# Four blocks of transformer layers on one core: a GpSimd wait moved three fetches later, long VectorE steps cut in pieces, and a static plan with other durations

## The chip, the cores and the metric

The kernel runs on one core of a Trainium2 chip. The metric is the device time of one launch in microseconds (us). Weights are rearranged on the host before the launch and are not timed. The core's engines are TensorE (PE in the rows), VectorE (DVE), ScalarE (ACT), GpSimd (POOL) and the queue of SyncE (SP), which only issues DMAs. Each engine runs its own list of instructions in order and waits on semaphores for the others.

## The reference

The input `x` has 2 x 1024 tokens of 256 features; a context has 2 x 154 tokens. Four layers follow each other, and each is a cross-attention and a feed-forward block, both with a layer norm in front and a residual sum behind:

```python
x = x + xattn0(ln(x), ctx);  x = x + ffn0(ln(x))   # ternary weights with a low-rank term
x = x + xattn1(ln(x), ctx);  x = x + ffn1(ln(x))   # 32 fetched expert rows per token, and a gated MLP
x = x + xattn2(ln(x), ctx);  x = x + ffn2(ln(x))   # rotary attention; 8 routed and 2 shared experts
x = x + xattn3(ln(x), ctx);  x = x + ffn3(ln(x))   # auto-correlation attention; 8 experts, top 2
```

Two parts matter here. In ffn0 the weights are made ternary on the chip:

```python
scale = clip(mean(abs(w), axis=1), 1e-5)
w_t = clip(round(w / scale), -1, 1) * scale
h = x @ w_fc_t.T + gate * (x @ v.T @ fast_b.T @ u.T);  y = relu(h) ** 2 @ w_proj_t.T
```

In ffn1 each token picks, for 4 heads, 8 of 4096 experts by two small top-8 searches, and then sums over its 32 experts:

```python
ew = silu(hidden . down_embed[indices]) * softmax(scores);  y = sum(ew * up_embed[indices])
```

## The kernel before, in words

The 2048 tokens are 4 chunks of 512, and a chunk is 4 tiles of 128 tokens (the partitions). All of `x` stays in SBUF as `x_sb`. The function `plan()` writes a list of work items for each engine: every item has an engine, a name, an assumed duration and the items that it needs. A list scheduler then goes through assumed time. When an engine is free it takes, of its items that are ready, the one with the longest remaining chain, and that order is the order in which the engine's instructions are written. Nothing is reordered on the chip. The table `DUR` holds assumed durations by item kind and overrides those in the `add` calls; an item kind that is not in it keeps the duration of its call. An item is never interrupted.

Items that the change touches:

- `tern`: ffn0's weights. VectorE makes them in three items. `tern(0)` (assumed 9 us) computes the scales and four of the 128-row blocks of `w_fc`, `tern(1)` (6 us) the other four, `tern(2)` (16 us) the two blocks of `w_proj`, and then adds the low-rank term to `w_fc` in eight steps, each after a TensorE product (L905) and a VectorE add (L1542). `tern(3)` is TensorE's 32 transposes with ScalarE's eight evictions (L920, L1264). The first product of ffn0, `h0(0,0)`, needs all eight evictions.
- `p1`: 16 short steps of an attention chunk, a TensorE product (L814) and a VectorE maximum (L1497) for each. TensorE may be two of them ahead. The attention's exponentials wait for the last one.
- `tk1` and `ix1` (`top1`, `rows1`, L1571 to L1603): VectorE's last steps of the routing of a chunk in ffn1. `ix1` is one item of 13.5 us, and ends with `rowid`, the indices, and `prob`, the weights.
- The gather. A unit `g` is 4 of the 32 expert rows of a tile of tokens; a chunk has 32 units, and there are 128 in all. Their rows go to a ring of 5 slots (20 rows of 2 x 256 values). For each unit GpSimd issues four indirect DMAs (`gf`, L1803), VectorE multiplies the first halves by the hidden state (`mu`, L1369), ScalarE sums each row (`th`, L1161), VectorE forms the four weights (`ew`, L1376 and L1377), VectorE adds the first three weighted rows to `x_sb` (`ad`, L1386 to L1388), ScalarE scales the fourth row (`sc`, L1170) and GpSimd adds it to `half_sum` (`ad`, L1817, or a copy, L1814). After eight units VectorE adds `half_sum` to `x_sb` (`ga`, L1394).
- `bo`: GpSimd adds an attention bias to the four tiles of a chunk (L1823).

A slot is refilled by `fetch(g)`. Before the first of its four DMAs GpSimd waits for VectorE's `ad` of unit g-5 (`f1_acc`, L1800) and for its own `ad` of that unit (`f1_half`, L1801). The item of GpSimd's own `ad` stands ahead of the fetch on the same engine, most often directly.

The chunks run in the order `A_ORDER`, (layer, chunk): (0,0), (0,1), (1,0), (1,1), (0,2), (0,3), (1,2), (1,3), (2,0) to (2,3). The gather of chunks 0 to 3 lies beside the attention and ffn of the chunks behind.

Of the kernel before, what the change touches and what calls it, by code (L numbers as in the profile page):

```python
# [10 lines left out]
P = 128  # L11
B, T, D = 2, 1024, 256
# [42 lines left out]
def columns(pack):  # L55
# [24 lines left out]
    DVE=dict(kv=3.2, N1=2.6, N3=1.0, p1=0.85, t=0.7, y=0.45, h0=0.78, y0=0.45, sm1=4.3, gu1=0.72, tk1=5.2, ix1=13.5, mu=1.27,  # L80
             ew=0.45, ad=1.7, ga=0.45, Q=6.2, lg2=5.5, gu2=0.72, y2=1.95, ks3=3.0, vs3=3.0, tp=4.0, y3=0.95, l3=1.2, lg3=7.0,
             be3=2.0, u3=1.1),
    POOL=dict(bo=3.1, gf=4.3, ad=0.82, bo3=6.0))
SIGNAL, LAND, BIAS_LATER = 0.22, 5.0, 10.0
# [3 lines left out]
LAST = NCH - 1  # L88

def plan():
# [113 lines left out]
    def ffn0(c, xt, prev):  # L205
        for m in range(8):
            p = add("PE", ("h0", c, m), 1.7, xt, *prev, c == 0 and ("ACT", ("tern", 3)), m > 1 and ("ACT", ("h0", c, m - 2)),
                    m and ("PE", ("h0", c, m - 1)))
            sq = add("ACT", ("h0", c, m), 1.3, p)
        use["xtf"] = p  # L210
        for i in range(TI):
            p = add("PE", ("y0", c, i), 3.2, sq, i > 1 and ("DVE", ("y0", c, i - 2)), i and ("PE", ("y0", c, i - 1)))
            out = add("DVE", ("y0", c, i), 0.43, p)
        return (out,)

    def ffn1(c, xt, prev):
# [11 lines left out]
        t2 = add("DVE", ("ix1", c), 13.0, a, c >= 2 and ("DVE", ("ga", UNITS * (c - 1) - 1)))  # L228
# [208 lines left out]
def build(nc, io):  # L437
# [10 lines left out]
    with ctx:  # L448
# [3 lines left out]
        def sem(name):  # L452
            return ctx.enter_context(nc.semaphore(name))
# [83 lines left out]
        def vrest(b):  # L537
# [27 lines left out]
        tn_w, tn_z, tn_zs, tn_u, tn_nat, tn_tp, tn_ev = (  # L565
            sem(s) for s in ("tn_w", "tn_z", "tn_zs", "tn_u", "tn_nat", "tn_tp", "tn_ev"))
# [166 lines left out]
        def _(eng):  # L733
# [162 lines left out]
            def tern(r):  # L896
                if r == 2:
                    eng.wait_ge(ld_f0, 16)
                    eng.wait_ge(tn_w, 1)
                    mm(psum[0:RANK, 6, 0:D], f0("fbt")[0:RANK, :], f0("v")[0:RANK, :], start=True, stop=True).then_inc(tn_z, 1)  # L900
                    eng.wait_ge(tn_zs, 1)
                    for m in range(8):
                        if m >= 2:
                            eng.wait_ge(tn_nat, m - 1)
                        mm(psum[:, 6 + m % 2, 0:D], utg[0:RANK, m * P:(m + 1) * P], lowv[0:RANK, :],  # L905
                           start=True, stop=True).then_inc(tn_u, 1)
                if r == 3:
                    eng.wait_ge(tn_nat, 8)
                    for t in range(8):
                        if t >= 2:  # L910
                            eng.wait_ge(tn_ev, t - 1)
                        for z in range(4):
                            if t < 4:
                                kt, m = t // 2, 4 * (t % 2) + z
                                src = fcnat[:, m, kt * P:(kt + 1) * P]
                            else:
                                mo = 4 * (t - 4) + z
                                m, o = mo // 2, mo % 2
                                src = projnat[:, o, m * P:(m + 1) * P]
                            ins = eng.transpose(psum[:, 6 + t % 2, z * P:(z + 1) * P], src, ident)  # L920
                        ins.then_inc(tn_tp, 1)
# [201 lines left out]
            def experts3(c, y):  # L1123
# [11 lines left out]
                for kt in range(KT):  # L1135
# [5 lines left out]
                    "w": weigh, "t": turn_back, "o": turn_out, "y": project_out, "tern": tern, "h0": hidden0, "y0": out0,  # L1141
# [8 lines left out]
        def _(eng):  # L1150
# [100 lines left out]
            def tern(r):  # L1251
# [3 lines left out]
                if r == 3:  # L1255
                    for t in range(8):
                        eng.wait_ge(tn_tp, t + 1)
                        if t < 4:
                            kt, m = t // 2, 4 * (t % 2)
                            dst = fc_t[:, kt, m * P:(m + 4) * P]  # L1260
                        else:
                            m = 2 * (t - 4)
                            dst = proj_t[:, m:m + 2, :].rearrange("p m n -> p (m n)")
                        act(dst, bank(6 + t % 2), ACT.Copy).then_inc(tn_ev, 1)  # L1264
# [93 lines left out]
        def _(eng):  # L1358
# [156 lines left out]
            def scales():  # L1515
                eng.wait_ge(ld_f0, 16)
                own.mark(eng.tensor_reduce(absum[:, 0:8], fcnat, AX.X, ALU.add, apply_absolute_value=True))
                own.link(eng.tensor_reduce(absum[:, 8:10], projnat, AX.X, ALU.add, apply_absolute_value=True))
                own.mark(ts(sclip[:, 0:8], absum[:, 0:8], 1.0 / D, 1e-5, ALU.mult, ALU.max))
                own.link(ts(sclip[:, 8:10], absum[:, 8:10], 1.0 / HID0, 1e-5, ALU.mult, ALU.max))  # L1520
                own.mark(ts(hi_th, sclip, 0.5, None, ALU.mult))
                own.link(ts(lo_th, sclip, -0.5, None, ALU.mult))
# [8 lines left out]
            def tern(r):  # L1531
                if r == 0:
                    scales()
                    ternary(range(0, 4))
                if r == 1:
                    ternary(range(4, 8))
                    ts(utg[0:RANK, :], utg[0:RANK, :], f0("gate")[0:RANK, :], None, ALU.mult).then_inc(tn_w, 1)
                if r == 2:
                    ternary(range(8, 10))
                    for m in range(8):  # L1540
                        eng.wait_ge(tn_u, m + 1)
                        tt(fcnat[:, m, :], fcnat[:, m, :], psum[:, 6 + m % 2, 0:D], ALU.add).then_inc(tn_nat, 1)  # L1542
# [37 lines left out]
            def rows1(c):  # L1580
                n = 16
                ex = ex1.rearrange("p (r k) -> p r k", r=n)
                for r in range(n):
                    own.mark(eng.max_index(pos[:, r * 8:r * 8 + 8], best[:, r, :], sums[:, r].rearrange("p i j -> p (i j)")))
                own.wait()
                own.mark(ts(pside[0], pos, 3, None, ALU.logical_shift_right))
                own.link(ts(pside[1], pos, 7, None, ALU.bitwise_and))
                for z in range(2):
                    own.mark(eng.tensor_copy(psidef[z], pside[z]))
                own.wait()  # L1590
                for z in range(2):
# [3 lines left out]
                    own.link(eng.reduce_sum(pick[z], eq.rearrange("p r k j -> p (r k) j"), AX.X))  # L1595
                own.link(stt(rowf, pick[0], float(NKEY), pick[1], ALU.mult, ALU.add))
                if c >= 2:
                    eng.wait_ge(f1_tile, TI * (c - 1))
                ts(rowid[c % 2][:, :], rowf, float(NEXP1 - 1), None, ALU.min).then_inc(f1_idx, 1)
                eng.wait_ge(f1_se, c + 1)  # L1600
                own.link(eng.reduce_sum(esum, ex, AX.X))
                own.link(eng.reciprocal(erec, esum))
                tt(prob[c % 2][:, :].rearrange("p (r k) -> p r k", r=n), ex, cast(erec.unsqueeze(2), [P, n, 8]), ALU.mult).then_inc(f1_idx, 1)  # L1603
# [153 lines left out]
            def experts3(c, y):  # L1757
# [5 lines left out]
                for r in range(2):  # L1763
# [9 lines left out]
                    "Q": project, "kv": kv, "p1": first_pass, "t": turn_back, "y": project_out, "tern": tern,  # L1773
# [8 lines left out]
        def _(eng):  # L1782
# [12 lines left out]
            def fetch(g):  # L1795
# [262 lines left out]
```

## Time and profile before

| | |
|---|---|
| median of 3 runs | 1874.29 us (1870.92 to 1875.08) |
| the profiled execution's own time | 1879.0 us |
| its span in the trace | 1877.2 us |
| mean granted TensorE clock, of full speed | 0.838 |
| busy: TensorE, VectorE, ScalarE, GpSimd | 74%, 60%, 44%, 36% |
| instructions | 19112 |

### The profile page before, as it was taken

Reading aid. Unit: us, or ns where it says so; the run is one execution under the profiler, and the core shown is the slowest. Engines: PE = TensorE matmul, PEld = TensorE weight load, DVE = VectorE, ACT = ScalarE, POOL = GpSimd, SP = SyncE. Lnnn points to the kernel's source line nnn. Section 1 sums busy time; section 2 is a strip of 40 time slices with the busy share of each in tenths; the row PEclk is TensorE's granted clock in tenths of the full one; section 3 lists DMA queues with packets and bytes.
Section 4 is the critical chain, followed back from the end, with each engine's and each line's share of the span. In section 5 each row is a group of like instructions: output and inputs, shape, how many; then the busy total and the mean of one; then the engine's idle time right before and its main releaser. Section 6 shows DMA issues by size and latency. Waiting matters only on the chain.

```text
span 1877.2 us, 19112 instructions
## 1 busy us (share of the span) xinstructions
PE 1398.0 (74%) x5858; PEld 698.8 (37%) x5858; DVE 1124.0 (60%) x3015; ACT 822.1 (44%) x2060; POOL 683.8 (36%) x705
## 2 busy tenths in 40 slices
PE   5779798757687785674664566766787996986898
PEld 3335344333243342323323332333353443442344
DVE  6322324458895767888969677677672245246265
ACT  2234344426667566574463537564832541120010
POOL 1000000045767777773774777777300010010000
PEclk7679798977888797787868778778878998989899
DMA  5000000054445557553545455555300031001000
GB/s 210 8 1 1 9 0 7 1 121 112 139 131 151 169 153 193 153 154 100 157 149 172 135 156 166 163 158 160 94 7 14 1 95 41 1 18 43 27 12 23
DMA packets 59382, 169.07 MB, mean 90 GB/s; under 512 B 15632, under 2 KB 20304, under 8 KB 58640
## 3 DMA queue, kind: packets, MB, share of 16 engines
q0 software_dynamic: 40960, 134.25, 25.8%
q1 hardware_dynamic: 18320, 33.61, 5.6%
q8 instruction: 46, 0.75, 0.2%
q14 instruction: 56, 0.46, 0.1%
HBM read 163.00 MB, written 4.82 MB: 89 GB/s over the span
## 4 chain that ended last, share of the span: by engine, by line
PE 39%; POOL 19%; DVE 17%; issue 11%; ACT 5%; DMA 5%; SPq 1%; another core or an unknown queue 1%; POOLq 0%; DVEq 0%; ACTq 0%
POOL bufR L1803 16%; PE psum L1136 5%; PE psum L814 3%; PE psum L1002 3%; POOL half_sum L1817 3%; PE psum L968 2%; DMA bufR<-in_table,rowid 2%; PE psum L1080 2%; PE psum L1059 2%; PE psum L893 2%; PE psum L1014 2%; PE psum L932 2%; PE psum L781 2%; ACT bufR L1235 2%; PE psum L940 2%
## 5 line engine op out<-in xcount | busy, mean ns | idle before, releaser
L1803 POOL DMA_INDIRECT bufR<-in_table,rowid x512 | 544.4, 1063 | 350.7 <-issue 138.5
L1161 ACT ACTIVATE bufR<-bufR 128x256 f32<-128x256 f32 x512 | 205.4, 404 | 140.0 <-DVE bufR L1369 131.9
L1369 DVE TENSOR_TENSOR bufR<-bufR 128x1024 f32<-128x1024 f32 x128 | 160.0, 1250 | 112.8 <-DMA bufR<-in_table,rowid 112.8
L1497 DVE TENSOR_REDUCE bufB<-psum 128x4 f32<-128x616 f32 x192 | 147.6, 793 | 110.1 <-PE psum L814 98.1
L814 PE MATMUL psum<-bufB 32*128 32x308 f32 x768 | 143.4, 566 | 84.9 <-DVE bufB L1497 46.8
L1002 PE MATMUL psum<-xtf,wf 128*128 128x512 f32 x320 | 162.4, 655 | 33.6 <-DVE x_sb L1652 15.8
L1014 PE MATMUL psum<-wf,bufR 128*128 128x256 f32 x320 | 97.7, 462 | 49.3 <-DVE bufR L1643 49.3
L1830 POOL TENSOR_TENSOR x_sb<-x_sb,wattn 128x256 f32<-128x256 f32 x16 | 11.0, 727 | 306.6 <-DMA wattn<-in_attn 178.4
L1823 POOL TENSOR_TENSOR x_sb<-x_sb,wattn 128x256 f32<-128x256 f32 x32 | 24.4, 796 | 266.8 <-DMA wattn<-in_attn 212.6
L814 PEld LDWEIGHTS psum<-bufB 32*128 32x128 f32 x768 | 58.1, 219 | 168.9 <-DVE bufB L1497 84.6
L1765 DVE SCALAR_TENSOR_TENSOR x_sb<-psum,bufR,x_sb 128x256 f32<-128x256 f32 x128 | 61.9, 484 | 81.2 <-PE psum L1136 74.8
L1817 POOL TENSOR_TENSOR half_sum<-half_sum,bufR 128x256 f32<-128x256 f32 x112 | 92.9, 829 | 46.2 <-ACT bufR L1170 43.9
L1002 PEld LDWEIGHTS psum<-xtf,wf 128*128 128x128 f32 x320 | 64.4, 210 | 118.4 <-issue 73.9
L1170 ACT ACTIVATE bufR<-bufR,ew 128x256 f32<-128x256 f32 x128 | 63.6, 501 | 96.0 <-DVE ew L1377 86.9
L968 PE MATMUL psum<-xtf,wf 128*128 128x512 f32 x128 | 79.4, 777 | 33.5 <-DVE bufR L1561 25.7
L1235 ACT ACTIVATE bufR<-psum 128x1024 f32<-128x1024 f32 x96 | 92.9, 1019 | 24.5 <-PE psum L840 24.2
L1014 PEld LDWEIGHTS psum<-wf,bufR 128*128 128x128 f32 x320 | 71.2, 231 | 80.5 <-issue 69.3
L1432 DVE TENSOR_TENSOR x_sb<-x_sb,psum 128x256 f32<-128x256 f32 x128 | 50.5, 416 | 81.0 <-PE psum L940 35.5
L838 PE MATMUL psum<-bufB 32*128 32x512 f32 x384 | 64.6, 746 | 44.3 <-ACT bufR L1235 37.4
L1161 ACT ACTIVATION_READ_ACCUMULATOR bufR<-bufR 128x1 f32 x512 | 96.7, 189 | 0.0
L1652 DVE SCALAR_TENSOR_TENSOR x_sb<-psum,bufR,x_sb 128x256 f32<-128x256 f32 x128 | 53.0, 476 | 42.1 <-PE psum L1014 41.5
L1388 DVE SCALAR_TENSOR_TENSOR x_sb<-bufR,ew,x_sb 128x256 f32<-128x256 f32 x128 | 72.0, 563 | 4.6
(239 smaller groups left out, 2549.8 us busy)
## 6 DMA issues: line engine op xcount, KB each, us to landing
bufR<-in_table,rowid POOLq DMA_INDIRECT x512
wf<-in_ffn SPq DMA_DIRECT2D x2, 2304.0 KB, 13.8
bufR<-in_ffn SPq DMA_DIRECT2D x1, 2696.5 KB, 16.0
wattn<-in_attn SPq DMA_DIRECT2D x4, 641.0 KB
wf<-in_rope SPq DMA_DIRECT2D x4, 512.0 KB, 5.7
bufB<-in_ffn SPq DMA_DIRECT2D x1, 2048.0 KB, 8.5
scr_corr<-bufR SPq DMA_DIRECT2D x16, 128.0 KB, 2.4
bufR<-scr_corr SPq DMA_DIRECT2D x4, 512.0 KB
```

The lines of the kernel that those rows point to most:

```text
L814: ins = mm(psum[:, 2 * (u % 2) + z, 0:PAR * S], q[r, g, i * P:(i + 1) * P], keysm[r, g, b, :, 0:S], start=True, stop=True)
L968: ins = mm(bank(6 + r), w1(name)[:, kt, m * P:(m + 1) * P], xtf[:, kt, :], start=kt == 0, stop=kt == KT - 1)
L1002: ins = mm(bank(6 + r), gu[:, kt, r, :], xtf[:, kt, :], start=kt == 0, stop=kt == KT - 1)
L1014: ins = mm(psum[:, (4 if c == LAST else 6) + i // 2, i % 2 * D:(i % 2 + 1) * D], hm2[:, GUS.index(m) % 7, i * P:(i + 1) * P], down2[:, m, ...
L1136: ins = mm(bank(unit_bank3(c, y)), xt_of("z", c)[:, kt, i * P:(i + 1) * P], we3[:, kt, e * 512:(e + 1) * 512], start=kt == 0, stop=kt == K ...
L1161: own.mark(act(row, row, ACT.Identity, accum_out=dots[:, g % 4, j:j + 1]))
L1235: act(probs[side][:, par:4:2, :], psum[:, 2 * side:2 * side + 2, :], ACT.Exp).then_inc(at_ex, 1)
L1369: tt(rows, rows, cast(xg[c % 2][:, i, :].unsqueeze(1), [P, GRP, D]), ALU.mult).then_inc(f1_mu, 1)
L1388: stt(x, ring[:, at + 2, D:2 * D], ew[:, g % 4, 2:3], x, ALU.mult, ALU.add).then_inc(f1_acc, 1)
L1497: eng.reduce_max(m4[:, i, :].rearrange("p (z r) -> p z r", z=BANDS)[:, 2 * side:2 * side + 2, PAR * g:PAR * g + PAR], psum[:, at:at + 2, 0 ...
L1803: eng.indirect_dma_start(ring[:, s * GRP + j, :], None, io["table"], bass.IndirectOffsetOnAxis(ap=rowid[c % 2][:, at + j:at + j + 1], axis ...
L1817: eng.tensor_tensor(half_sum[:, :], half_sum[:, :], up, ALU.add).then_inc(f1_half, 1)
```

## The change: what it does, and the diff

1. In `fetch`, the wait for `f1_half` moves from ahead of the slot's four DMAs to ahead of the fourth. GpSimd's own `ad` reads only the fourth row of the slot. The wait for `f1_acc` stays ahead of the first.
2. VectorE's long items are cut: `tern(0)` into four pieces of scales, `tern(1)` into eight ternary blocks, `tern(2)` into two, the eight low-rank adds become items `low` of their own on TensorE and VectorE, and `tern(3)` becomes eight items on TensorE and ScalarE, of which the four for `w_proj` no longer need the low-rank adds. `ix1` becomes four pieces (4.4, 3.6, 3.6 and 1.9 us). Arithmetic and operand shapes of the big steps stay the same; the scales are computed by block, with 16 instructions for 6.
3. In `DUR`, GpSimd's `gf` goes from 4.3 to 5.0 us, `bo` from 3.1 to 3.7, `ad` from 0.82 to 0.8, and the assumed landing time `LAND` of a gather from 5.0 to 4.0. So the orders of all engines are made anew.

```diff
-    POOL=dict(bo=3.1, gf=4.3, ad=0.82, bo3=6.0))
-SIGNAL, LAND, BIAS_LATER = 0.22, 5.0, 10.0
+    POOL=dict(bo=3.7, gf=5.0, ad=0.8, bo3=6.0))
+SIGNAL, LAND, BIAS_LATER = 0.22, 4.0, 10.0
...
+TERN_STEPS = (4, 8, 2)
...
-        t2 = add("DVE", ("ix1", c), 13.0, a, c >= 2 and ("DVE", ("ga", UNITS * (c - 1) - 1)))
+        for n in range(4):
+            t2 = add("DVE", ("ix1", c, n), (4.4, 3.6, 3.6, 1.9)[n], a, c >= 2 and ("DVE", ("ga", UNITS * (c - 1) - 1)))
...
-            add("PE", ("tern", 2), 6.0, ("DVE", ("tern", 1)))
-            add("ACT", ("tern", 2), 0.6, ("DVE", ("tern", 1)))
+            p = add("PE", ("tern", 2), 0.6, ("DVE", ("tern", 1, TERN_STEPS[1] - 1)))
+            add("ACT", ("tern", 2), 0.6, p)
         if r < 3:
-            add("DVE", ("tern", r), (9.0, 6.0, 16.0)[r], ("SP", ("in", "f0")), r and ("DVE", ("tern", r - 1)))
-    add("PE", ("tern", 3), 5.0, ("DVE", ("tern", 2)))
-    add("ACT", ("tern", 3), 5.0, ("DVE", ("tern", 2)))
+            for n in range(TERN_STEPS[r]):
+                last = add("DVE", ("tern", r, n), (1.7, 1.6, 2.9)[r], ("SP", ("in", "f0")))
+    for m in range(8):
+        p = add("PE", ("low", m), 0.5, ("ACT", ("tern", 2)), m > 1 and ("DVE", ("low", m - 2)))
+        last = add("DVE", ("low", m), 0.5, p, last)
+    for t in range(8):
+        p = add("PE", ("tern", 3, t), 0.65, ("DVE", ("low", 7)) if t < 4 else ("DVE", ("tern", 2, 1)), t > 1 and ("ACT", ("tern", 3, t - 2)))
+        add("ACT", ("tern", 3, t), 0.65, p)
...
                 if g >= SLOTS:
                     eng.wait_ge(f1_acc, g - SLOTS + 1)
-                    eng.wait_ge(f1_half, g - SLOTS + 1)
                 for j in range(GRP):
+                    if g >= SLOTS and j == GRP - 1:
+                        eng.wait_ge(f1_half, g - SLOTS + 1)
                     eng.indirect_dma_start(ring[:, s * GRP + j, :], None, io["table"],
```

In the code of the engines `tern`, `low` and `rows1` take the number of the piece and run that part alone; a piece of `rows1` begins with a wait for VectorE's own earlier instructions.

## Rows read from the trace of the kernel before

**Rows 1.** The page: busy time, and the chain of waits by engine

```profile
PE 1398.0 (74%) x5858; PEld 698.8 (37%) x5858; DVE 1124.0 (60%) x3015; ACT 822.1 (44%) x2060; POOL 683.8 (36%) x705
PE 39%; POOL 19%; DVE 17%; issue 11%; ACT 5%; DMA 5%; SPq 1%; another core or an unknown queue 1%; POOLq 0%; DVEq 0%; ACTq 0%
```

**Rows 2.** Busy time of each engine in stretches of the span

```profile
core 0: us, PE busy (x) PEld busy (x) DVE busy (x) ACT busy (x) POOL busy (x), PEclk, DMA share, GB/s
81.00:121.00 40.00, 26.86 (x124) 7.46 (x125) 0.56 (x2) 14.55 (x18) 0.00 (x0) 0.63 0.00 1
121.00:392.00 271.00, 228.70 (x1054) 113.86 (x1052) 106.58 (x353) 110.66 (x163) 5.54 (x8) 0.91 0.01 3
392.00:1345.00 953.00, 631.60 (x2496) 323.18 (x2496) 727.95 (x1873) 553.31 (x1647) 658.46 (x656) 0.79 0.54 151
1345.00:1877.00 532.00, 459.38 (x2009) 224.90 (x2008) 241.52 (x680) 125.65 (x199) 11.03 (x16) 0.92 0.10 26
```

**Rows 3.** The chain of waits, 570 to 573 us: start, length, what

```profile
570.05 0.75 POOL half_sum L1817
...
570.83 0.02 POOLq L1801
570.85 0.72 issue
571.57 0.96 POOL bufR L1803
```

**Rows 4.** The chain of waits, first and last of its 64 stops at L1801

```profile
556.18 0.02 POOLq L1801
...
1327.68 0.02 POOLq L1801
```

**Rows 5.** Timeline: start, length, and idle time before it in brackets

```profile
735.69 0.95 POOL L1803 DMA_INDIRECT bufR<-in_table,rowid  x1 [0.30 <-issue]
...
740.67 1.21 DVE L1369 TENSOR_TENSOR bufR<-bufR 128x1024 f32<-128x1024 f32 x1
...
740.88 1.83 POOL L1803 DMA_INDIRECT bufR<-in_table,rowid  x1 [0.16 <-issue]
```

**Rows 6.** Waits on GpSimd and VectorE: us in total, times, longest

```profile
POOL bufR L1803 <- DVE x_sb L1388: 36.8, 19, 13.1
DVE bufR L1369 <- DMA bufR<-in_table,rowid: 112.8, 49, 5.6
```

**Rows 7.** Line 1803's 512 indirect DMAs: ns min/median/max; page: busy us, mean ns

```profile
L1803 POOL DMA_INDIRECT bufR<-in_table,rowid x512: 942/955/2002, 392.4 to 1332.5; - x171
...
L1803 POOL DMA_INDIRECT bufR<-in_table,rowid x512 | 544.4, 1063 | 350.7 <-issue 138.5
```

**Rows 8.** Timeline of VectorE, the first attention's `p1` steps

```profile
31.70 0.80 DVE L1497 TENSOR_REDUCE bufB<-psum 128x4 f32<-128x616 f32 x1
...
71.59 1.51 DVE L1497 TENSOR_REDUCE bufB<-psum 128x4 f32<-128x616 f32 x2 [10.83 <-PE psum L814]
...
80.54 0.80 DVE L1497 TENSOR_REDUCE bufB<-psum 128x4 f32<-128x616 f32 x1 [0.51 <-PE psum L814]
```

**Rows 9.** Groups of VectorE's instructions, 20 to 60 us: busy us, mean ns

```profile
L1529 DVE TENSOR_TENSOR bufR<-bufR 128x256 f32<-128x256 f32 (+1 forms) x10 | 5.9, 585 | 0.3
L1527 DVE TENSOR_SCALAR bufR<-bufR 128x256 f32<-128x256 f32 (+1 forms) x10 | 4.9, 490 | 0.3
L1528 DVE TENSOR_SCALAR bufR<-bufR 128x256 f32<-128x256 f32 (+1 forms) x10 | 4.9, 486 | 0.0
```

**Rows 10.** The chain of waits, first product of `h0(0,0)`

```profile
139.03 1.95 PE psum L932 x4
```

**Rows 11.** Timelines of VectorE and GpSimd around the third routing

```profile
860.02 0.29 DVE L1603 TENSOR_TENSOR prob<-bufR 128x128 f32<-128x128 f32 x1
...
863.96 0.95 POOL L1817 TENSOR_TENSOR half_sum<-half_sum,bufR 128x256 f32<-128x256 f32 x1 [14.40 <-ACT bufR L1170]
...
873.46 1.13 POOL L1803 DMA_INDIRECT bufR<-in_table,rowid  x1 [0.80 <-POOL half_sum L1817]
```

More of the change, by code:

```diff
@@ L206, in ffn0 @@
         for m in range(8):
-            p = add("PE", ("h0", c, m), 1.7, xt, *prev, c == 0 and ("ACT", ("tern", 3)), m > 1 and ("ACT", ("h0", c, m - 2)),
+            p = add("PE", ("h0", c, m), 1.7, xt, *prev, c == 0 and ("ACT", ("tern", 3, 7)), m > 1 and ("ACT", ("h0", c, m - 2)),
                     m and ("PE", ("h0", c, m - 1)))
@@ L894, in project_out, with tern @@
                 ins.then_inc(at_wo, 1)
-            def tern(r):
+            def tern(r, t=None):
                 if r == 2:
@@ L900, in tern @@
                     mm(psum[0:RANK, 6, 0:D], f0("fbt")[0:RANK, :], f0("v")[0:RANK, :], start=True, stop=True).then_inc(tn_z, 1)
-                    eng.wait_ge(tn_zs, 1)
[L902 to L921, printed above, removed]
@@ new lines, in tern @@
+                    return
+                if t < 4:
+                    eng.wait_ge(tn_nat, 8)
+                else:
+                    eng.wait_ge(tn_proj, 1)
+                if t >= 2:
+                    eng.wait_ge(tn_ev, t - 1)
+                for z in range(4):
+                    if t < 4:
+                        kt, m = t // 2, 4 * (t % 2) + z
+                        src = fcnat[:, m, kt * P:(kt + 1) * P]
+                    else:
+                        mo = 4 * (t - 4) + z
+                        m, o = mo // 2, mo % 2
+                        src = projnat[:, o, m * P:(m + 1) * P]
+                    ins = eng.transpose(psum[:, 6 + t % 2, z * P:(z + 1) * P], src, ident)
@@ L923, in hidden0, with low @@
+                ins.then_inc(tn_tp, 1)
+            def low(m):
+                if m == 0:
+                    eng.wait_ge(tn_zs, 1)
+                else:
+                    eng.wait_ge(tn_u, m)
+                if m >= 2:
+                    eng.wait_ge(tn_nat, m - 1)
+                mm(psum[:, 6 + m % 2, 0:D], utg[0:RANK, m * P:(m + 1) * P], lowv[0:RANK, :], start=True, stop=True).then_inc(tn_u, 1)
             def hidden0(c, m):
@@ L1249, in turn_out, with tern @@
                 act(ot[:, g, :], bank(g), ACT.Copy).then_inc(at_ot, 1)
-            def tern(r):
+            def tern(r, t=None):
                 if r == 2:
@@ L1254, in tern @@
                     act(lowv[0:RANK, :], psum[0:RANK, 6, 0:D], ACT.Copy).then_inc(tn_zs, 1)
[L1255 to L1264, printed above, removed]
+                    return
+                eng.wait_ge(tn_tp, t + 1)
+                if t < 4:
+                    kt, m = t // 2, 4 * (t % 2)
+                    dst = fc_t[:, kt, m * P:(m + 4) * P]
+                else:
+                    m = 2 * (t - 4)
+                    dst = proj_t[:, m:m + 2, :].rearrange("p m n -> p (m n)")
+                act(dst, bank(6 + t % 2), ACT.Copy).then_inc(tn_ev, 1)
             def hidden0(c, m):
@@ L1513, in project_out, with scales @@
                 add_x(c, i, psum[:, (2, 3, 0, 1)[i], 0:D]).then_inc(at_x, 1)
[L1515 to L1522, printed above, removed]
+            def scales(n):
+                if n == 0:
+                    eng.wait_ge(ld_f0, 16)
+                rows, src = ((slice(0, 4), fcnat[:, 0:4]), (slice(4, 8), fcnat[:, 4:8]), (slice(8, 9), projnat[:, 0:1]), (slice(9, 10), projnat[:, 1:2]))[n]
+                own.link(eng.tensor_reduce(absum[:, rows], src, AX.X, ALU.add, apply_absolute_value=True))
+                own.link(ts(sclip[:, rows], absum[:, rows], 1.0 / (D if n < 2 else HID0), 1e-5, ALU.mult, ALU.max))
+                own.mark(ts(hi_th[:, rows], sclip[:, rows], 0.5, None, ALU.mult))
+                own.link(ts(lo_th[:, rows], sclip[:, rows], -0.5, None, ALU.mult))
             def ternary(rows):
@@ L1529, in ternary, with tern, low @@
                     own.link(tt(nat, tplus[:, 0:n_], tminus[:, 0:n_], ALU.subtract))
-            def tern(r):
+            def tern(r, n):
                 if r == 0:
-                    scales()
-                    ternary(range(0, 4))
+                    scales(n)
                 if r == 1:
-                    ternary(range(4, 8))
-                    ts(utg[0:RANK, :], utg[0:RANK, :], f0("gate")[0:RANK, :], None, ALU.mult).then_inc(tn_w, 1)
+                    ternary((n,))
+                    if n == 7:
+                        ts(utg[0:RANK, :], utg[0:RANK, :], f0("gate")[0:RANK, :], None, ALU.mult).then_inc(tn_w, 1)
                 if r == 2:
[L1539 to L1542, printed above, removed]
+                    ternary((8 + n,))
+                    if n == 1:
+                        eng.sem_inc(tn_proj, 1)
+            def low(m):
+                eng.wait_ge(tn_u, m + 1)
+                tt(fcnat[:, m, :], fcnat[:, m, :], psum[:, 6 + m % 2, 0:D], ALU.add).then_inc(tn_nat, 1)
             def out0(c, i):
@@ L1578, in top1, with rows1 @@
                 tt(ex, best, cast(best[:, :, 0:1], [P, n, 8]), ALU.subtract).then_inc(f1_sc, 1)
-            def rows1(c):
+            def rows1(c, part):
                 n = 16
                 ex = ex1.rearrange("p (r k) -> p r k", r=n)
-                for r in range(n):
-                    own.mark(eng.max_index(pos[:, r * 8:r * 8 + 8], best[:, r, :], sums[:, r].rearrange("p i j -> p (i j)")))
                 own.wait()
[L1586 to L1591, printed above, removed]
+                if part == 0:
+                    for r in range(n):
+                        own.mark(eng.max_index(pos[:, r * 8:r * 8 + 8], best[:, r, :], sums[:, r].rearrange("p i j -> p (i j)")))
+                    own.wait()
+                    own.mark(ts(pside[0], pos, 3, None, ALU.logical_shift_right))
+                    own.link(ts(pside[1], pos, 7, None, ALU.bitwise_and))
+                    for z in range(2):
+                        own.mark(eng.tensor_copy(psidef[z], pside[z]))
+                if part in (1, 2):
+                    z = part - 1
                     own.link(tt(eq.rearrange("p r k j -> p (r k) j"), cast(psidef[z].unsqueeze(2), [P, P, 8]),
```

29 lines of the change are left out of this document (15 added, 14 removed).

## The prediction

> **What bounds the kernel now.** I read the page's totals and its chain of waits first. No engine is full: TensorE is busy 74% of the span, and it holds 39% of the chain; GpSimd is busy 36% but holds 19%, and most of the chain's 11% "issue" lies between GpSimd's instructions [rows 1]. So the limit changes with the stretch. The stretches show three parts [rows 2]. From 121 to 392 us TensorE is busy 229 of 271 us. From 392 to 1345 us, the gather, GpSimd is busy 658 of 953 us, VectorE 728 and TensorE 632. After 1345 us TensorE is busy 459 of 532 us, which is its work and little else. A hole stands ahead of them: from 81 to 121 us VectorE does 0.56 us of work in 40.
>
> Then I read the chain where it runs on GpSimd. A unit looks like this [rows 3]: the fourth fetch of a slot ends (0.95 us), the own row is added (0.75), the queue stops at L1801, which is the wait for that very add, and the next fetch begins 0.72 us after the wait has ended. Between two fetches with no such wait the gap is 0.30 us. The chain passes such a stop 64 times, all between 556 and 1328 us [rows 4].
>
> **Part 1, the moved wait.** It adds and removes no instruction: 123 fetches (units 5 to 127) wait for the same semaphore, three DMAs later. At that place GpSimd has still to write the three descriptor sets ahead, about 3 x 0.95 us, while the add is long done, so the wait should cost nothing there. Behind it on GpSimd's queue stand the fourth fetch and the next `ad`; both are behind the same three fetches anyway. The gap ahead of the first fetch is now 0.02 + 0.02 + 0.72, about 0.77 us. What is left of it is seen once: behind a bias add, whose results no fetch waits for, a fetch starts after 0.16 us [rows 5]. The cautious bound is the 0.30 us of the usual gap. So a unit gains between 0.47 and 0.61 us, and I take 0.55, nearer to the row that shows the same sequence of instructions. 64 x 0.55 = 35 us on the chain, with 30 and 39 as the bounds.
>
> Not all of it survives, because what is late next is the other wait, for VectorE's three rows of the unit five back: it already ended the idle time of 19 of the 123 fetches, 36.8 us in all [rows 6]. With GpSimd faster by 0.55 us a unit this wait binds more often. I let the same share go, 15%, and keep 30 us. VectorE has room in these stretches: it waited 112.8 us, in 49 waits, for a fetch to land [rows 6], and that wait is what shrinks.
>
> One row speaks against a denser GpSimd. The median fetch takes 955 ns and the longest 2002 [rows 7]. The one at 740.88 us took 1.83 while VectorE's multiply L1369 was running [rows 5]. The mean of all 512 is 1063 ns [rows 7], so whatever lengthens them costs 512 x 0.108 = 55 us now. The number of multiplies and fetches does not change. A gather that is 5% shorter meets 5% more of them, 3 us at most, inside the 5 us that I gave up. The Trainium skill (SBUF — State Buffer, the shared port pair) says that VectorE and GpSimd share one port pair, as an exclusive lock, and that whoever comes second blocks for the other's whole instruction. It also infers that a two-input VectorE operation should leave the writing of descriptors alone. By the first sentence a moved fetch gains less than its gap whenever it starts into a multiply; by the second there would be no loss at all. The rows lean to the first.
>
> **Part 2a, `tern` in pieces.** The first attention's 16 `p1` steps start at about 32 us and end at 81.3 us [rows 8]. When nothing stands between them, ten take from 71.59 to 81.34 us, 0.98 us each [rows 8]; 16 would take 16 us. Between them lie the ternary blocks (ten triples, 5.9 + 4.9 + 4.9 = 15.7 us [rows 9]), the low-rank adds, the transposes, and other short items. The exponentials wait for the last `p1`, and VectorE then waits for TensorE through the hole [rows 2]. Cut in pieces the ternary work can go into the hole. The planner assumes a gap of 0.3 us after every second `p1`, and being greedy puts a piece of 1.6 us there. Eight such pieces cost 8 x 1.3 = 10 us, and for the short items that stay I leave 3. So the last `p1` would end at 32 + 16 + 10 + 3 = 61 us in place of 81, 20 us earlier. The rest, less than the whole of the ternary blocks' 15.7 us with the low-rank adds, fits into the 40 us hole of VectorE and is done ahead of `h0(0,0)`, which starts at 139 us now [rows 10] and would at 119. I take 18 us, because ScalarE's eight evictions now stand between exponentials. The bounds are 5 us (pieces ordered badly, TensorE's transposes in the way) and 25 us. From 121 to 392 us TensorE is 84% busy with work that does not depend on this, so that stretch moves earlier as a whole, and with it the first fetch at 392 us.
>
> The scales need 16 short instructions for 6, about 0.6 us more of VectorE, in an idle stretch: nothing.
>
> **Part 2b, `ix1` in pieces.** The third routing ended at 860.02 us. Meanwhile GpSimd sat 14.40 us waiting for a weighted row whose weights VectorE had not formed, and 1.60 us more for VectorE's rows; the first fetch of the new chunk came at 873.46 us, so the indices had been ready for 13.2 us [rows 11]. The longest wait for VectorE's rows, 13.1 us [rows 6], is the same thing at the fourth routing. Pieces let `ew` and `ad` of the old chunk in between. But if they go ahead, the indices come later by as much, and the slack is only 13.2 us. Of the 29 us of stalls I count 8.
>
> **Part 3, the plan.** The old plan assumed 4.3 + 0.82 = 5.1 us for a unit. The trace has 940 us from the first to the last fetch [rows 7], 7.3 us for each of 128 units, and a quiet one takes 0.77 + 4 x 0.955 + 3 x 0.30 + 0.75 = 6.2 us [rows 3, 7]. The new plan assumes 5.8 us, where the quiet unit will be 6.2 - 0.55 = 5.7 us. VectorE's list should hold fewer multiplies that come up before their rows have landed (the 112.8 us), and items behind them wait less. What that is worth the trace can't show, since the order of every engine is new: between +15 us and -25 us. I take +3 us, a loss: GpSimd's longer assumed time lengthens the remaining chain of all that leads to the gather, and so draws TensorE's other work behind it.
>
> **The sum.** -30 - 18 - 8 + 3 = -53 us. From the profiled execution's 1879.0 us that gives 1826 us; the median of the runs shown is 4.7 us lower, 1874.3, which gives 1821. I say 1823 us, 2.7% faster.
>
> **The rivals.**
>
> *VectorE takes GpSimd's place (about 1855 us).* VectorE is busy 76% of the gather, TensorE 66% [rows 2]. If two thirds of the 35 us turn into waits for VectorE's rows or for indices, and `tern` gives 8 us: -12 - 8 = -20. For it: the 19 waits and the slack of 13.2 us. Against it: the 112.8 us in which VectorE waits for fetches.
>
> *All parts join (about 1796 us).* The full 35 us, 20 us for `tern`, and the stalls at the third and fourth routing gone, 25 us: -80. Two-input blocking and the new order speak against it.
>
> *Slower: TensorE's work moves behind the gather (about 1885 us).* After 1345 us TensorE is 86% busy [rows 2], so what the new plan puts behind the last fetch is added to the end. The place is `ffn2` of the chunks 0 to 2, which stands beside the last third of the gather. With a gain of 53 us elsewhere, the change loses from 53 x 0.86 = 46 us of moved TensorE work on; 56 us (an `ffn2` of ten experts at the plan's 3.8 + 1.8 us) give 56 / 0.86 - 53 = +12. Against it: the plan values the rest of the chain of that work too.
>
> *Nothing happens (about 1874 us).* The 0.72 us might be the start of a fetch behind any other instruction, not the price of the wait, and `tern` might be shifted, not hidden. The 0.16 us behind a bias add [rows 5] speaks against it, though it is one row.
>
> **How the numbers follow.** My forecast, -35 to -70 us around -53 (1804 to 1840 us): 0.50. VectorE in GpSimd's place (1840 to 1870): 0.26. All parts join (below 1804): 0.12. No change: 0.04. Slower: 0.08. The range 1790 to 1862 us leaves out the slower end of the second case, the far end of the third, and the last two: about 0.2. About 0.2% (4 us) is what a measurement of this kernel can tell from no change; so faster 0.88, same 0.04, slower 0.08.
>
> **What would show it.** Right: the gap ahead of a slot's first fetch is 0.16 to 0.30 us instead of 0.77, the fourth has no longer gap than the others, a quiet unit takes 5.7 us; the last `p1` of the first attention ends near 61 us and ternary blocks lie between 60 and 120 us; the first fetch comes near 374 us; the last one near 1285 us in place of 1332; VectorE waits for landings less than 112.8 us. Wrong: the gap stays near 0.7 us or moves to the fourth fetch; waits of GpSimd for L1388 well above 36.8 us; or more than 532 us between the end of the gather and the end of the span.

## The result and the profile after

The changed kernel takes 1788.9 us (median of 4 runs, 1785.18 to 1798.64); the kernel before took 1874.68 us beside it. The ratio is 0.9546, with a 95% interval of 0.9499 to 0.9593: 86 us faster, where I had forecast 53. It lies 1 us below my range. The direction was right, and so were the mechanisms of the moved wait and of the cut `tern`. The size was not: the terms of the moved wait and of `tern` were too small, and that of the plan had the wrong sign.

The page of the changed kernel, busy time and the chain by engine, as in [rows 1]:

```profile
PE 1384.3 (77%) x5858; PEld 687.2 (38%) x5858; DVE 1121.7 (63%) x3025; ACT 810.9 (45%) x2050; POOL 689.3 (39%) x705
PE 44%; DVE 18%; POOL 14%; issue 9%; ACT 7%; DMA 5%; SPq 1%; another core or an unknown queue 1%; DVEq 0%; POOLq 0%; ACTq 0%
```

The same work is done in 89 us less of span, and GpSimd's share of the chain has fallen from 19% to 14%. TensorE's matmuls took 14 us less (1384.3 for 1398.0 us), at a mean granted clock of 0.855 for 0.838. Whether any of the gain comes by that clock, or the clock rose because the gather was shorter, no run separates. The gather in stretches of the changed kernel, columns as in [rows 2], and its 512 fetches, as in [rows 7]:

```profile
60.00:99.00 39.00, 36.23 (x167) 13.72 (x167) 7.88 (x13) 18.21 (x26) 0.00 (x0) 0.71 0.00 1
371.00:1250.00 879.00, 619.89 (x2472) 310.59 (x2472) 722.81 (x1867) 542.58 (x1636) 663.84 (x656) 0.80 0.59 164
```

```profile
L1821 POOL DMA_INDIRECT bufR<-in_table,rowid x512: 942/957/1998, 370.9 to 1234.3; - x171
```

The first fetch comes at 370.9 us for 392.4, the last at 1234.3 for 1332.5. So 21.5 us are gained ahead of the gather, and 77 us in it; 9 us are given back behind it (1787.8 - 1234.3 = 553.5 us from the last fetch to the end, for 1877.2 - 1332.5 = 544.7).

A unit on GpSimd in the changed kernel, from its timeline (start, length, idle time before it in brackets):

```profile
569.11 0.73 POOL L1835 TENSOR_TENSOR half_sum<-half_sum,bufR 128x256 f32<-128x256 f32 x1
570.00 1.13 POOL L1821 DMA_INDIRECT bufR<-in_table,rowid  x1 [0.16 <-issue]
571.44 1.00 POOL L1821 DMA_INDIRECT bufR<-in_table,rowid  x1 [0.30 <-issue]
572.74 1.39 POOL L1821 DMA_INDIRECT bufR<-in_table,rowid  x1 [0.31 <-issue]
574.44 0.95 POOL L1821 DMA_INDIRECT bufR<-in_table,rowid  x1 [0.30 <-issue]
```

The gap behind GpSimd's own add is 0.16 us, the value of [rows 5], for 0.77. The fourth fetch, which now carries the wait, has the usual 0.30. So it is in the whole trace: of the 123 units that refill a slot, 108 have a first gap below 0.25 us, where before 112 had one between 0.6 and 0.85, and no fourth fetch has a gap above 0.35 us.

The first attention on VectorE in the changed kernel, pairs of `p1` maxima (L1508) with one ternary block (L1538 to L1540) between them, the last `p1`, and the wait that is left of the hole:

```profile
36.79 1.50 DVE L1508 TENSOR_REDUCE bufB<-psum 128x4 f32<-128x616 f32 x2
38.22 0.40 DVE L1538 TENSOR_SCALAR bufR<-bufR 128x256 f32<-128x256 f32 x1
38.53 0.41 DVE L1539 TENSOR_SCALAR bufR<-bufR 128x256 f32<-128x256 f32 x1
38.98 0.43 DVE L1540 TENSOR_TENSOR bufR<-bufR 128x256 f32<-128x256 f32 x1
39.44 1.50 DVE L1508 TENSOR_REDUCE bufB<-psum 128x4 f32<-128x616 f32 x2
...
56.49 0.80 DVE L1508 TENSOR_REDUCE bufB<-psum 128x4 f32<-128x616 f32 x1 [0.67 <-PE psum L821]
...
99.05 0.26 DVE L1515 RECIPROCAL bufR<-psum 128x16 f32<-128x16 f32 x1 [21.85 <-PE psum L883]
```

The last of the 16 steps ends at 57.3 us for 81.3 [rows 8]. What is left of the ternary work runs behind it, until 77.2 us, in what was the hole.

Waits of GpSimd and VectorE in the changed kernel, as in [rows 6]:

```profile
POOL half_sum L1835 <- ACT bufR L1182: 32.9, 9, 7.7
POOL bufR L1821 <- DVE x_sb L1399: 27.8, 8, 8.1
```

```profile
DVE bufR L1380 <- DMA bufR<-in_table,rowid: 46.5, 27, 5.1
```

VectorE's waits for landings fell from 112.8 to 46.5 us, and GpSimd waits no longer than before for VectorE's rows: 27.8 us, for 36.8.

### The profile page after: what moved, and what is told of

It is laid out like the page before. It is cut to its first block, busy times and chain, and to the rows that moved or that the text cites. A ratio compares the mean times of both kernels' runs of the same rounds, so it can differ in the third digit from the quotient of the medians.

```text
span 1787.8 us, 19004 instructions
## 1 busy us (share of the span) xinstructions
PE 1384.3 (77%) x5858; PEld 687.2 (38%) x5858; DVE 1121.7 (63%) x3025; ACT 810.9 (45%) x2050; POOL 689.3 (39%) x705
## 4 chain that ended last, share of the span: by engine, by line
PE 44%; DVE 18%; POOL 14%; issue 9%; ACT 7%; DMA 5%; SPq 1%; another core or an unknown queue 1%; DVEq 0%; POOLq 0%; ACTq 0%
POOL bufR L1821 12%; PE psum L1148 5%; PE psum L1014 4%; PE psum L821 3%; PE psum L944 3%; PE psum L980 2%; PE psum L1092 2%; DVE bufB L1508 2%; PE psum L1026 2%; PE psum L845 2%; PE psum L870 2%; PE psum L952 2%; ACT bufR L1247 2%; PE psum L873 2%; PE psum L1071 2%
## 5 line engine op out<-in xcount | busy, mean ns | idle before, releaser
L1821 POOL DMA_INDIRECT bufR<-in_table,rowid x512 | 550.7, 1076 | 284.4 <-issue 126.3
L1508 DVE TENSOR_REDUCE bufB<-psum 128x4 f32<-128x616 f32 x192 | 147.7, 794 | 93.8 <-PE psum L821 91.0
L1380 DVE TENSOR_TENSOR bufR<-bufR 128x1024 f32<-128x1024 f32 x128 | 160.2, 1252 | 48.3 <-DMA bufR<-in_table,rowid 46.5
L1014 PEld LDWEIGHTS psum<-xtf,wf 128*128 128x128 f32 x320 | 62.2, 203 | 118.6 <-issue 72.6
L1026 PE MATMUL psum<-wf,bufR 128*128 128x256 f32 x320 | 89.8, 433 | 18.1 <-DVE bufR L1660 18.0
L1026 PEld LDWEIGHTS psum<-wf,bufR 128*128 128x128 f32 x320 | 66.2, 215 | 47.0 <-issue 37.6
L870 PE MATMUL psum<-bufB 128*128 128x512 f32 x96 | 61.5, 727 | 20.0 <-ACT bufB L1253 19.9
```

The lines of the kernel that those rows point to most:

```text
L870: mm(bank(at), vrest(b)[:, G, :], prest[:, G % 2, :], start=True, stop=False, skip_group_check=True)
L1014: ins = mm(bank(6 + r), gu[:, kt, r, :], xtf[:, kt, :], start=kt == 0, stop=kt == KT - 1)
L1026: ins = mm(psum[:, (4 if c == LAST else 6) + i // 2, i % 2 * D:(i % 2 + 1) * D], hm2[:, GUS.index(m) % 7, i * P:(i + 1) * P], down2[:, m, ...
L1380: tt(rows, rows, cast(xg[c % 2][:, i, :].unsqueeze(1), [P, GRP, D]), ALU.mult).then_inc(f1_mu, 1)
L1508: eng.reduce_max(m4[:, i, :].rearrange("p (z r) -> p z r", z=BANDS)[:, 2 * side:2 * side + 2, PAR * g:PAR * g + PAR], psum[:, at:at + 2, 0 ...
```

## The experiments

There are four parts: W, the moved wait; T, `tern` in pieces; X, `ix1` in pieces; P, the plan's durations. Each run is compared with the kernel before on its own chip; a gain in us is (1 - ratio) times that kernel's time there (1863 to 1873 us). Brackets hold the 95% interval.

**W alone.**

```diff
-                    eng.wait_ge(f1_half, g - SLOTS + 1)
                 for j in range(GRP):
+                    if g >= SLOTS and j == GRP - 1:
+                        eng.wait_ge(f1_half, g - SLOTS + 1)
```

> Only the moved wait, with the plan and the items of the kernel before. The gather became 74 us shorter in the changed kernel, where I had forecast 35. Theory A (the wait was priced too low): every one of the 123 fetches gains 0.61 us, and not only the 64 at which the chain stopped, so this run alone is 55 to 70 us faster, ratio 0.963 to 0.971. Theory B (the wait is worth what I forecast, about 30 us, and the rest comes from the new orders): ratio 0.981 to 0.986. In both, the gap ahead of a slot's first fetch is 0.16 us.

Ratio 0.9774 (0.9736 to 0.9811), 42 us (35 to 49). The timeline of GpSimd in this run:

```profile
564.94 0.74 POOL L1818 TENSOR_TENSOR half_sum<-half_sum,bufR 128x256 f32<-128x256 f32 x1
565.83 0.96 POOL L1804 DMA_INDIRECT bufR<-in_table,rowid  x1 [0.16 <-POOL half_sum L1818]
...
571.28 0.74 POOL L1818 TENSOR_TENSOR half_sum<-half_sum,bufR 128x256 f32<-128x256 f32 x1
572.58 0.96 POOL L1804 DMA_INDIRECT bufR<-in_table,rowid  x1 [0.56 <-DVE x_sb L1388]
```

The result lies between both theories. The gap falls to 0.16 us in one unit; in the next VectorE's third row is late and leaves 0.56. The whole account, against the second trace of before (below): the gather, from the first to the last fetch, takes 879.7 us for 925.7, 46 less. The gaps ahead of fetches fell by 67 us. Of these 21 were given back: the fetches took 6 us longer, GpSimd's adds 4 us, and the waits of these adds, for the weighted row and for `ga`, 12 us.

**T and X together, P alone, and everything but W.**

```diff
-    POOL=dict(bo=3.1, gf=4.3, ad=0.82, bo3=6.0))
-SIGNAL, LAND, BIAS_LATER = 0.22, 5.0, 10.0
+    POOL=dict(bo=3.7, gf=5.0, ad=0.8, bo3=6.0))
+SIGNAL, LAND, BIAS_LATER = 0.22, 4.0, 10.0
```

These four lines are P. T and X are the diff's other plan and VectorE lines.

> Only the pieces of tern and ix1, old wait and old assumed durations of GpSimd. Theory A: 21 us from tern, as the first fetch showed (370.89 us for 392.40), and no more than 8 from ix1: ratio 0.984 to 0.990. Theory B: the pieces also let the gather go on, 40 us or more together, ratio below 0.979.

> Only the assumed durations of GpSimd and the landing time. Theory A: worth nothing by itself, ratio 0.995 to 1.008. Theory B: with old wait and long items VectorE already waits less for landings (112.8 us before), 15 to 35 us, ratio 0.981 to 0.992.

> The changed kernel with the wait put back ahead of the first fetch. It takes the same order of all engines as the changed kernel. Theory A: 55 to 70 us slower than the changed kernel, about 1850 us, ratio to the kernel before 0.982 to 0.990. Theory B: 30 us slower, about 1820 us, ratio 0.969 to 0.973.

T and X: 0.9844 (0.9793 to 0.9894), 29 us, as in theory A. P: 0.9914 (0.9886 to 0.9942), 16 us, against both "nothing" and my forecast of a small loss. That is the ratio of theory B but not its path: VectorE waits 112.5 us for landings, as before. All but W: 0.9803 (0.9757 to 0.9849), 37 us, between its two theories, as W alone. The changed kernel has 0.9546, so on top of the others W is worth a factor of 0.9546 / 0.9803 = 0.974, 49 us, with both intervals taken together 36 to 61.

**The kernel before once more.** No edit.

> The kernel before, unchanged, for a second trace of it beside traces of the same chip. The runs of the moved wait alone came out 2.3% faster, while its trace ends 60 us (3.2%) ahead of the first trace of before. Theory M (the first trace of before was a long execution): ratio 0.998 to 1.002, and a span of 1855 to 1870 us. Theory N: the span is again 1877 us, and the traces measure something else than the timed runs.

Ratio 1.0004 (0.9979 to 1.003), span 1862.4 us. These are theory M's numbers, but "a long execution" explains only a part of the 15 us between the spans. The runs beside the first trace have a median of 1874 us, those beside the second 1864 to 1865, and only 5 us are the first execution's own excess over its median. So the trace of the changed kernel, taken beside runs of 1874.68 us, is compared with the first trace, and those of W, T, X and P with the second.

The chain in this second trace stops at L1801 78 times, where the first had 64 [rows 4]: the count on which I built the term moves by a fifth from one trace of the same kernel to another. In eight further traces, of other kernels with the old wait, it was 49 to 89 times.

**T alone and X alone.**

> Only tern in pieces. The pieces together gave a ratio of 0.984, 29 us. Theory A: the 21 us by which the first fetch comes earlier reach the end whole, ratio 0.987 to 0.990, and the gather takes as long as before. Theory B: tern alone gives less, because the new order brings new waits, ratio above 0.991.

> Only ix1 in pieces. My forecast's term: GpSimd's stalls at the third and fourth routing shrink and 8 us are gained, ratio 0.996. Rival: the routing itself ends later by as much, ratio 0.998 to 1.003. In the first case GpSimd's waits for ScalarE's weighted row and VectorE's rows, 80.7 us before, fall to under 60.

T: 0.9865 (0.9832 to 0.9899), 25 us; the first fetch at 371.7 us for 394.2 in the second trace of before, and the gather about as long as before (920.2 us from the first to the last fetch for 925.7). What was gained early, 22.5 us, reaches the end, within the interval. X: 0.9953 (0.9932 to 0.9973), 9 us. GpSimd's waits for the weighted row and VectorE's rows are 36.1 + 34.7 = 70.8 us, for 39.3 + 33.3 = 72.6 in the second trace of before, where I had expected less than 60. So my 8 us were met, but not by my path: the sum of these waits hardly fell. The longest one for VectorE's rows did, from 12.4 to 6.6 us, but the longest for the weighted row did not (14.7 us, for 13.2). Where the 9 us come from stays open.

The four parts alone multiply to 0.9774 x 0.9865 x 0.9953 x 0.9914 = 0.951, beside 0.9546 for the whole (0.9520 when run again, below). Within the intervals, about 0.006 for such a product, they neither cover each other nor need each other.

**What in the plan's part counts.** First GpSimd's three durations alone, with the landing time as before; then, with all of P's other values, the fetch at 3.6 and at 5.7 us.

```diff
-    POOL=dict(bo=3.1, gf=4.3, ad=0.82, bo3=6.0))
+    POOL=dict(bo=3.7, gf=5.0, ad=0.8, bo3=6.0))
...
+    POOL=dict(bo=3.7, gf=3.6, ad=0.8, bo3=6.0))
...
+    POOL=dict(bo=3.7, gf=5.7, ad=0.8, bo3=6.0))
```

> Only GpSimd's three assumed durations, with the old landing time of 5.0. The plan's part gave 0.9914. If the durations of GpSimd's items are what counts, the ratio is 0.988 to 0.994 and GpSimd's waits for the weighted row and VectorE's rows are near 38 us, as with the whole of that part; if the landing time counts, the ratio is 0.997 to 1.003 and they are near 80.

> The kernel before with the new bias duration and landing time, and 3.6 us assumed for a fetch, still further below the traced 5.4 us (four fetches with their gaps) than the old 4.3. The plan's part alone gave 0.9914 and its GpSimd durations alone 0.9866. Theory F (the plan gains because its durations come nearer the trace): the ratio is 1.005 or more and GpSimd's waits for the weighted row and VectorE's rows are over 80 us. Theory L (any new order is a draw, and this one was lucky): the ratio lies anywhere from 0.985 to 1.015, without relation to the durations.

> The same with 5.7 us for a fetch, so that a unit takes 6.5 us in the plan; the trace has 6.6 us as the median unit. Theory F: at least as fast as with 5.0, ratio 0.980 to 0.992, GpSimd's waits for the weighted row and VectorE's rows under 45 us. Theory L: anywhere from 0.985 to 1.015.

Ratios: 0.9866 (0.9823 to 0.991) for the durations alone; 1.0078 (1.005 to 1.0105) with 3.6 us, and 0.9834 (0.9807 to 0.9861) with 5.7 us. With the durations alone GpSimd's two waits are 42.7 us, near the 38 that I expected, so the landing time does not explain the gain. In the order 3.6, 4.3 (before), 5.0, 5.7 us the ratios are 1.0078, 1, 0.9914, 0.9834: each step closer to the traced unit of 6.6 us is faster, by about the same amount. The steps aren't quite clean: the 4.3 of before goes with the old landing time and bias duration, and 5.0 us with the old landing time gave 0.9866, half a step away from 0.9914. The two outer points were called in advance, in sign and about in size; the gain at 5.0 was not. GpSimd's waits in three of these kernels, the second trace of before, P alone, and 5.7 us:

```profile
POOL half_sum L1817 <- ACT bufR L1170: 39.3, 7, 13.2
POOL bufR L1803 <- DVE x_sb L1388: 33.3, 15, 12.4
```

```profile
POOL half_sum L1817 <- ACT bufR L1170: 20.8, 5, 7.4
POOL bufR L1803 <- DVE x_sb L1388: 17.6, 14, 3.4
POOL half_sum L1814 <- DVE x_sb L1394: 4.4, 1, 4.4
```

```profile
POOL half_sum L1817 <- ACT bufR L1170: 12.6, 3, 6.4
POOL bufR L1803 <- DVE x_sb L1388: 7.0, 9, 0.8
POOL half_sum L1814 <- DVE x_sb L1394: 6.1, 1, 6.1
```

Their sums are 72.6, 42.8 and 25.7 us. In return GpSimd waits some 12 us for the indices of one routing with P and with 5.7 us, which it did not before. With 3.6 us the waits for the weighted row and VectorE's rows are 59.0 us, and not the more than 80 that I expected; but 21.9 us for `ga` (L1394) and 15.3 for indices come to them. With all of these waits counted the sums are 96, 73, 55 and 37 us for 3.6 us, before, P and 5.7 us, and the gather takes 950, 926, 908 and 889 us from the first to the last fetch. The two fall together: GpSimd, the engine that paces most of the gather, is kept waiting less by VectorE and ScalarE. VectorE's waits for landings, which I had named as the gain, don't follow so well: 147.0 us with 3.6, 109.0 in the second trace of before, 112.5 with P and 76.1 with 5.7.

**The plan on top of the other parts.** The changed kernel with the old P, then with 5.4 us for a fetch; then the changed kernel again beside 5.8 and 6.4 us.

```diff
-    POOL=dict(bo=3.7, gf=5.0, ad=0.8, bo3=6.0))
+    POOL=dict(bo=3.7, gf=5.4, ad=0.8, bo3=6.0))
```

> The changed kernel with the old assumed durations of GpSimd and the old landing time. If the parts add up, the plan is worth 0.9 to 1.3% here too: ratio to the kernel before 0.963 to 0.968. If the moved wait makes the old durations fit (a quiet unit is 5.6 us now, the plan had 5.1), the plan is worth less than 0.4%: ratio 0.954 to 0.959.

> The changed kernel with 5.4 us for a fetch instead of 5.0, a unit of 6.2 us in the plan; the changed kernel's trace has a median unit of 6.22 us. Theory F: as fast as the changed kernel or faster, ratio 0.948 to 0.955. Theory L: a draw, ratio 0.945 to 0.970.

> The changed kernel, unchanged, beside the next two on one chip. Ratio 0.950 to 0.959 as first measured.

> The changed kernel with 5.8 us for a fetch, a unit of 6.6 us in the plan, above its traced 6.2. If the plan only has to be no faster than the chip: as fast as with 5.4 (0.9512), 0.948 to 0.954. If it has to match: slower than with 5.4, 0.955 or more.

> The changed kernel with 6.4 us for a fetch, a unit of 7.2 us in the plan, 1 us above the trace. Theory F (the match counts, both ways): slower than with 5.4 by 0.5% or more. Rival (a slow GpSimd in the plan is always right, since it puts VectorE's gather work late): again 0.948 to 0.954.

| `gf` assumed, us | 4.3 (old P) | 5.0 (the change) | 5.4 | 5.8 | 6.4 |
|---|---|---|---|---|---|
| ratio to before | 0.9605 | 0.9520 | 0.9512 | 0.9585 | 0.9661 |
| interval | 0.9575 to 0.9634 | 0.9479 to 0.9562 | 0.9482 to 0.9543 | 0.9544 to 0.9627 | 0.9633 to 0.9688 |

The old plan's 0.9605 lies between its two theories, in neither window. On top of the other parts the plan is worth 0.6 to 0.9%, by which of the two ratios of the changed kernel is taken (0.9546 or 0.9520); alone it was 0.9%.

With the wait moved the traced median unit is 6.2 us, which is 5.4 + 0.8, and the times have their lowest point at 5.0 and 5.4, which can't be told apart. Above it they rise again, at 6.4 us clear of the intervals and at 5.8 only just, so a plan that only assumes a slow GpSimd isn't enough. With 6.4 us this is what GpSimd waits for:

```profile
POOL half_sum L1832 <- DVE x_sb L1405: 79.4, 12, 11.8
```

L1405 is `ga`, VectorE's sum at the end of a tile, which comes too late in its list; in the changed kernel this wait is 2.9 us. The version with 5.4 us is the lowest ratio of all, but not below the change by more than its interval.

**Where the own wait may stand.** W with the wait ahead of the second fetch.

```diff
-                    if g >= SLOTS and j == GRP - 1:
+                    if g >= SLOTS and j == 1:
```

> The kernel before with the wait for GpSimd's own add ahead of the second fetch of a slot instead of the first (in the change: ahead of the fourth). Theory Q (the 0.72 us behind the wait is the queue starting again, and it only has to lie under something): the first fetch runs 0.96 us beside it, so nothing is seen, the second's gap stays 0.30 us and the gain is that of the moved wait alone, ratio 0.974 to 0.981. Theory D (the add has first to be complete, and its results settled, before another three fetches have passed): a gap of 0.5 us or more turns up ahead of the second fetch, ratio above 0.985.

Ratio 0.9753 (0.9724 to 0.9783), as W. The timeline of GpSimd in this run:

```profile
564.34 0.74 POOL L1818 TENSOR_TENSOR half_sum<-half_sum,bufR 128x256 f32<-128x256 f32 x1
565.24 0.96 POOL L1804 DMA_INDIRECT bufR<-in_table,rowid  x1 [0.16 <-POOL half_sum L1818]
566.50 0.95 POOL L1804 DMA_INDIRECT bufR<-in_table,rowid  x1 [0.30 <-issue]
```

No new gap, in this unit or in any other: 4 of the 128 second fetches have a gap above 0.35 us, as in both traces of before. That is theory Q's result: what costs is that nothing else is queued on GpSimd when its own wait ends, and a single fetch of 0.96 us covers it. Three give no more than one. Whether the 0.6 us is the queue starting again, as theory Q has it, or the end of the add becoming known late, isn't shown: one fetch would cover either.

## Why the prediction was right in its direction and wrong in its size

| term | forecast, us | bounds | measured, the part alone, us |
|---|---|---|---|
| part 1, the moved wait | -30 | -30 to -39, less a share | -42 (-35 to -49); on top of the others -49 (-36 to -61) |
| part 2a, `tern` | -18 | -5 to -25 | -25 (-19 to -31) |
| part 2b, `ix1` | -8 | | -9 (-5 to -13) |
| part 3, the plan | +3 | -25 to +15 | -16 (-11 to -21) |
| sum | -53 | -35 to -70 | -92 for the four; the whole change -86 |

**Part 1.** The mechanism was right in each point: 0.16 us behind the add, no gap ahead of the fourth fetch, no cost of the wait in its new place. The step that failed is "64 x 0.55 = 35", and then "I let the same share go, 15%". The price was 0.61 us, what [rows 5] showed; I had shaded it. The 64 stops were those of one trace, and the second trace of before has 78. The count itself was the wrong one: 112 of the 123 first gaps were 0.6 to 0.85 us long in the first trace, and W took 67 us out of the gaps ahead of fetches. The share that went was too small as well, 21 of these 67 us, 31%. The two errors pull in opposite directions, so that 30 came as near to 42 as it did is partly luck. Why stops off the chain count too is argued and not shown: where the chain leaves GpSimd for a while, GpSimd arrives earlier at the place where it returns.

**The port.** I left up to 3 us for a denser GpSimd. The median fetch took 955 ns before and 957 after, and the mean 1063 and 1076: 512 x 0.013 = 7 us more on GpSimd. That is more than I allowed, and small beside the gain. The start times tell where the long fetches come from. One more pair beside that of [rows 5], from the first trace of before:

```profile
732.09 1.23 DVE L1369 TENSOR_TENSOR bufR<-bufR 128x1024 f32<-128x1024 f32 x1 [0.19 <-DMA bufR<-in_table,rowid]
732.15 1.99 POOL L1803 DMA_INDIRECT bufR<-in_table,rowid  x1 [0.30 <-issue]
```

**Part 2a.** Right in place and order, down to one block after each pair. The step mis-sized is "I take 18 us, because ScalarE's eight evictions now stand between exponentials". The last `p1` came at 57.3 us instead of my 61, 24 us earlier than before, and little of that is lost behind it: the trace has the first fetch 21.5 us earlier, 23.3 against the second trace of before. So the evictions can't have cost much more than 2.5 us.

**Part 2b.** The size was right, the reading was not: the longest stall for VectorE's rows was halved, the one for the weighted row was not, and their sum hardly fell. That the 8 us were met is luck as far as the runs tell.

**Part 3.** This is the step with the wrong sign: "I take +3 us, a loss: GpSimd's longer assumed time lengthens the remaining chain of all that leads to the gather, and so draws TensorE's other work behind it." That effect exists. From the last fetch to the end it takes 553.5 us for 544.7, 9 us longer in the changed kernel (549.8 when traced again), and 541.7 in the kernel with all parts but the plan's. It is the one sign of being wrong on my list that came. But it is outweighed by what I had left out of the sum because "the trace can't show" it: lists made with a unit of 5.1 us keep GpSimd waiting on a chip whose unit takes 6.6. The evidence was in my rows: GpSimd's 36.8 us for VectorE's rows [rows 6] and the 14.40 us at the third routing [rows 11]. I booked them under `ix1`, as long items. With P alone, `ix1` still whole, the longest of these waits are 7.4 and 3.4 us, so they were mostly the old plan's; 12 us of what that saved went into the wait for indices.

**The rivals.** "VectorE takes GpSimd's place" happened in small part: VectorE is busy 723 of 879 us, 82%, and in W GpSimd's adds waited 12 us longer. But GpSimd waited only 27.8 us for VectorE's rows. "All parts join" is the time that came, and I gave it 0.12. It didn't come by that rival's sum: it had 35, 20 and 25 us for the wait, `tern` and `ix1` and nothing for the plan, and the runs show 42, 25, 9 and 16. The slower rival is seen only as the 9 us.

## What to carry to other kernels

An engine that waits for its own last instruction can pay for it even though that instruction has ended: here GpSimd lost 0.61 us each time. Put that wait behind at least one other instruction that doesn't need it; one was enough here. In a kernel whose instruction lists come from a planner, try the start-to-start spacing in the trace, gaps included, as the assumed duration of the pacing engine's unit. With the wait moved, shorter and longer ones were both slower, by 1 to 2% for 1 us; with the old wait only shorter ones were tried, down to 4.4 for 6.6 us. Take counts on the chain from two traces before building a sum on them, and count the same event off the chain too. Where parts were expected to get in each other's way, here they did not by more than the intervals.

## What the runs showed of the hardware

GpSimd started an indirect DMA 0.16 us after the end of an add for which nothing had waited in between, 0.30 us after another indirect DMA, and 0.77 us after an add whose end its queue had waited for. That a fetch comes sooner behind an add than behind another fetch was not expected.

A fetch that began while VectorE's 128x1024 multiply ran, and was lengthened by it, ended 0.82 us after the multiply (0.82 to 0.85 us, 71 fetches of the first trace of before, 78 of W alone); a multiply that began while a fetch ran kept its 1.22 us.

The profiled executions of one unchanged kernel differed by 15 us (1877.2 and 1862.4 us), some 10 of which are seen in all runs beside them: this kernel's medians were 1863 to 1865 us on two chips and 1873 on a third. The mean granted TensorE clock was 0.838 and 0.842, and 0.855 to 0.860 in the changed kernel. What makes one chip or execution slower stays open.
